# Beta folded into one decay exponent, the T-products evacuated by ScalarE, and a new order of the work on all engines of a fused delta-rule block

## The reference: what is computed

```
x = x + 0.5 * ffn(layernorm(x))       # r = sigmoid(xr Wr'), out = r * (relu(xk Wk')^2 Wv'), xr and xk mix each token with its predecessor
x = x +       attn(layernorm(x))
x = x + 0.5 * ffn(layernorm(x))
```

```
beta = sigmoid(h Wb');  g = -exp(A_log) * softplus(h Wa' + dt_bias)
S  = S * exp(g_t)
dv = (v_t - k_t S) * beta_t
S  = S + k_t (outer) dv
o  = q_t S
out = (o * rsqrt(mean(o*o) + 1e-5) * norm_w * silu(h Wg')) Wo'
```

## Time and profile before

| what | us |
|---|---|
| runs | 1873.60, 1883.21, 1891.46; median 1883.21 |
| the profiled execution's own time | 1883.35 |
| its span, first to last instruction | 1881.6 |
| busy PE, DVE, ACT, POOL | 1739.6, 1521.0, 1089.1, 438.4 |
| mean granted clock of TensorE | 0.965 of full |

### The profile page before, as it was taken

The page is one execution under the profiler, slowest core; times in us unless marked ns, Lnnn a source line. Parts: engine busy times, 40 slices in busy tenths (PEclk is TensorE's granted clock), DMA queues, the critical chain, the costliest instruction groups (busy, mean ns, idle before and its releaser), DMA issues.

```text
span 1881.6 us, 101829 instructions
## 1 busy us (share of the span) xinstructions
PE 1739.6 (92%) x45312; PEld 1486.7 (79%) x45312; DVE 1521.0 (81%) x4294; ACT 1089.1 (58%) x2002; POOL 438.4 (23%) x357
## 2 busy tenths in 40 slices
PE   5699999999999999999999999999999999999986
PEld 4587888787888788888888888888888878888775
DVE  4877889887888988888887888898788898887852
ACT  5556665555665565666565666555566555565533
POOL 0222221222221222222121222122222222222200
PEclk9889999999999999999999999999999999999877
DMA  3000000000000000000000000000000000000000
GB/s 113 2 3 4 15 14 4 15 14 15 15 15 9 9 15 15 15 15 15 3 15 14 15 15 15 9 9 14 15 15 15 9 9 9 9 9 10 9 9 13
DMA packets 21590, 26.50 MB, mean 14 GB/s; under 512 B 2209, under 2 KB 20769, under 8 KB 21153
## 3 DMA queue, kind: packets, MB, share of 16 engines
q1 hardware_dynamic: 21152, 19.99, 3.3%
HBM read 11.59 MB, written 8.39 MB: 11 GB/s over the span
## 4 chain that ended last, share of the span: by engine, by line
PE 53%; DVE 28%; issue 11%; ACT 1%; POOL 1%; DVEq 1%; ACTq 0%; POOLq 0%
PE ps L244 23%; PE ps L226 11%; PE ps L235 8%; DVE CV L1067 6%; DVE prod L1082 4%; DVE TZ L1083 3%; PE ps L219 2%; PE ps L400 2%; DVE T L1102 2%; PE ps L212 2%; DVE st L1035 2%; DVE XR L1056 1%; PE ps L357 1%; PE ps L461 1%; PE ps L372 1%
## 5 line engine op out<-in xcount | busy, mean ns | idle before, releaser
L1067 DVE SCALAR_TENSOR_TENSOR CV<-ps,cw,CV 128x256 f32<-128x256 f32 x576 | 250.8, 477 | 22.2 <-ACT CV L686 15.0
L244 PE MATMUL ps<-QE,S 64*64 64x16 f32 x4096 | 251.6, 209 | 2.0 <-ACT S L631 1.3
L244 PE MATMUL ps<-WP,V 64*64 64x16 f32 x4096 | 250.1, 208 | 0.0
L244 PEld LDWEIGHTS ps<-QE,S 64*64 64x64 f32 x4096 | 216.4, 138 | 35.0 <-issue 31.2
L244 PEld LDWEIGHTS ps<-WP,V 64*64 64x64 f32 x4096 | 217.4, 138 | 0.0
L244 PEld LDWEIGHTS ps<-WP,KD 64*64 64x64 f32 x4096 | 127.1, 137 | 36.5 <-DVE WP L1125 22.7
L1082 DVE TENSOR_TENSOR prod<-A,TZ 128x30 f32<-128x30 f32 (+7 forms) x480 | 139.0, 290 | 13.3
L967 POOL TENSOR_TENSOR OSQ<-OSQ,SQ 128x512 f32<-128x512 f32 x32 | 40.6, 1269 | 459.8 <-ACT OSQ L840 459.8
L244 PEld LDWEIGHTS ps<-SA,M 32*32 32x32 f32 x8192 | 91.0, 108 | 68.9 <-issue 34.3
L244 PE MATMUL ps<-SA,M 32*32 32x16 f32 x8192 | 117.9, 181 | 28.8 <-DVE SA L1096 18.4
L244 PE MATMUL ps<-KQI,K 64*64 64x48 f32 x4096 | 141.8, 221 | 1.4 <-DVE CV L1067 0.7
(11 more groups left out here) (152 smaller groups left out, 4055.4 us busy)
## 6 DMA issues: line engine op xcount, KB each, us to landing
X<-in_x SPq DMA_DIRECT2D x32, 256.0 KB, 2.9
out_x<-X SPq DMA_DIRECT2D x32, 256.0 KB, 2.3
KQI<-in_blocks SPq DMA_DIRECT2D x2, 256.0 KB, 4.2
w_r_ffn<-in_wT_r_ffn SPq DMA_DIRECT2D x1, 256.0 KB, 3.3
w_k_ffn<-in_wT_k_ffn SPq DMA_DIRECT2D x1, 256.0 KB, 3.5
w_v_ffn<-in_wT_v_ffn SPq DMA_DIRECT2D x1, 256.0 KB, 4.4
w_k<-in_wT_k SPq DMA_DIRECT2D x1, 256.0 KB, 4.3
w_q<-in_wT_q SPq DMA_DIRECT2D x1, 256.0 KB, 4.5
```

The source lines that it names most:

```text
L244: last = mm(ps[rows, o:o + n], stat[rows, pk].rearrange("p s c -> p (s c)"), mov[rows], **flags)
L1067: last = stt(d4[:, m], src, cw[:, i, m, tap:tap + 1], d4[:, m], ALU.mult, ALU.add)
```

## The change

What is computed stays the same. The parts:

- **One exponent.** `beta_diag` (GpSimd) writes log beta on the diagonal of a tile LD, and `stat1` becomes two operations, `stat0` and a subtraction, so that the statistic for `decay_steps` holds both g and log beta. `beta_in`, the tile EA, the second exp, `b_diag`, `b_reduce` and `beta_log` go. E now holds beta times the decay.
- **The gram step** multiplies both k·k and k·q by the same E in one 256-column operation (GK replaces AT and KP).
- **T on ScalarE.** `t_out0` and `t_out1` move from VectorE to ScalarE, three activations of 256 columns each, reading PSUM; no scaling by beta is left, two of the three scale by a 0/1 column.
- **Softplus.** `soft_exp` on ScalarE is now a chain of five: Abs, Exp, Identity (+1), Ln, Exp. VectorE keeps four operations of 64 columns and one of 32 (`soft_low`, `soft_part`, `soft_log`, `soft_max`, `gates`); the reciprocal goes.
- **Merged evacuation.** `d_out0` to `d_out3` write one tile MQ (384 columns in one operation) where M2 and QE took two; MQ has two buffers.
- **Finer segments.** The solve is issued as single multiplies and subtracts with other work between them, `t_product` and `b_product` in four parts, `o_product` in eight.
- **New order** on all engines but SyncE, and a new table `PS` of banks. ScalarE changes its table set twice in a step.

```diff
-PS = {"xt1": 2, "yt": 6, "xt3": 2, "r1": 0, ... "wo": 1, "g": 2, "dd": 5, ... "d1": 3, ... "t0": 0, "t1": 6, ...}
+PS = {"xt1": 5, "yt": 4, "xt3": 1, "r1": 2, ... "wo": 5, "g": 6, "dd": 4, ... "d1": 4, ... "t0": 4, "t1": 6, ...}
 # TensorE
-            def t_product1(g):
+            def t_product(g, q):
+                if q == 0:
+                    pe.wait_ge(s["tp"], g + 1)
...
+                for pk in range(q * RING, (q + 1) * RING):
+                    last = pairs(bk * BANK + pk % C * U, U, T2, pk, GK[:, pk, C:], start=True, stop=True)
...
             def d_product1(g):
...
+                if g < GROUPS - 2:
+                    pe.wait_ge(s["yt"], g + 3)
...
             def wo(g):
                 pe.wait_ge(s["ot"], g + 1)
...
-            def beta_in(g):
-                pe.wait_ge(s["lb"], g + 1)
-                pe.wait_ge(s["e"], g + 1)
-                for ub in range(M * B):
...
-                    last = mm(ps[:, o:o + P], LB[:, c0:c0 + P], ident, start=False, stop=(ub == M * B - 1), skip_group_check=True)
 # ScalarE
             def soft_exp(g):
...
+                own.done(af(ez[:], Z[:], ACT.Abs))
+                own.settle()
+                own.done(af(ez[:], ez[:], ACT.Exp, scale=-1.0))
+                own.settle()
+                own.done(af(uz[:], ez[:], ACT.Identity, bias=one))
+                own.settle()
+                own.done(af(lu[:], uz[:], ACT.Ln))
+                own.settle()
+                af(ru[:], lu[:], ACT.Exp, scale=-1.0).then_inc(s["ez"], 1)
...
+            def t_out0(g):
+                act.wait_ge(s["t_ps"], 4 * g + 2)
...
+                for h in range(2):
+                    own.done(af(WP[g % 2][:, rows, h * C:(h + 1) * C], src[:, :, C:U], ACT.Copy, scale=slot[:, h:h + 1]))
+                nc.scalar.copy(WP[g % 2][:, rows, U:], src[:, :, 0:C]).then_inc(s["wp"], 1)
 # GpSimd
+            def beta_diag(g):
+                pool.wait_ge(s["sp"], 5 * g + 5)
...
+                tt(packs(LD[:]), along(cz[:, BH:2 * BH]), over_packs(diag), ALU.mult).then_inc(s["ld"], 1)
             def stat1(g):
...
+                tt(ST[:], ST[:], LD[:], ALU.subtract).then_inc(s["stat1"], 1)
 # VectorE
             def d_out0(g):
...
-                own.done(tt(packs(QE[g % 2][:])[:, rows], packs(QP[:])[:, rows], src[:, :, U:], ALU.subtract))
-                tt(M2[:, rows].rearrange("p k s c -> p k (s c)"), GI2[:, rows], src[:, :, 0:U], ALU.subtract).then_inc(s["mt"], 1)
+                tt(MQ[g % 2][:, rows], GQ[:, rows], src, ALU.subtract).then_inc(s["mt"], 1)
             def gram0(g):
...
-                own.done(tt(packs(AT[:])[:, rows], src[:, :, 0:C], packs(EA[:])[:, rows], ALU.mult))
-                own.done(tt(KP[:, rows, C:U], src[:, :, C:U], packs(E[:])[:, rows], ALU.mult))
-                own.done(tt(KP[:, rows, 0:C], k_tok, along(packs(E[:])[:, rows, C - 1]), ALU.mult))
+                own.done(tt(GK[:, rows, 0:U].rearrange("p k (s c) -> p k s c", s=2), src[:, :, 0:U].rearrange("p k (s c) -> p k s c", s=2),
+                            vw(packs(E[:])[:, rows], [C, RING], [0, 2], [1, C]), ALU.mult))
+                own.done(tt(GK[:, rows, U:], k_tok, along(packs(E[:])[:, rows, C - 1]), ALU.mult))
```

More of the change, by code:

```diff
@@ L373, in q_proj, with b_product @@
                 last.then_inc(s["q_ps"], 1)
[L375 removed]
+            def b_product(g, q):
+                if q == 0:
+                    pe.wait_ge(s["wp"], 2 * g + 2)
+                    pe.wait_ge(s["vt"], g + 1)
+                if g and q == 0:
+                    pe.wait_ge(s["ch_s"], 8 * g)
                 w2 = WP[g % 2][:, :, 0:U].rearrange("p k (s c) -> p k s c", s=2)
[L377 removed]
+                for n in range(2 * q, 2 * q + 2):
                     for ub in range(M * B):
@@ L894, in _ @@
             ln_exp_set()
-            for step in range(GROUPS + 4):
-                on(square_k, step - 2)
+            for step in range(GROUPS + 5):
+                on(norm3, step - 5)
+                on(relu1, step - 1)
+                on(soft_exp, step - 2)
+                on(xt3, step - 5)
+                on(v_slots, step - 4)
+                silu_set()
+                on(gate, step - 2)
+                on(s_slots, step - 4)
+                on(relu3, step - 5)
+                on(silu_k, step - 2)
+                on(square_k, step - 2)
+                on(silu_v, step - 3)
+                on(tanh1, step - 1)
+                on(tap_v, step - 2)
+                on(tanh3, step - 5)
+                on(gates_wide, step - 2)
+                on(silu_q, step - 2)
@@ L897, in _ @@
                 ln_exp_set()
-                on(soft_exp, step - 2)
-                silu_set()
-                on(tanh1, step - 1)
+                on(k_root, step - 2)
+                on(rstd2, step - 1)
                 on(o_square, step - 4)
-                on(silu_v, step - 2)
+                on(norm2, step - 1)
+                on(exp_q, step - 2)
+                on(halo_y, step - 1)
+                on(t_out0, step - 3)
                 on(halo3, step - 4)
-                ln_exp_set()
@@ L905, in _ @@
                 on(o_root, step - 4)
-                on(halo1, step)
-                on(rstd1, step)
-                on(soft_ln, step - 2)
-                on(k_root, step - 2)
-                on(gates_wide, step - 2)
-                on(halo_y, step - 1)
-                on(rstd2, step - 1)
+                on(yt, step - 1)
+                on(square_q, step - 2)
+                on(t_out1, step - 3)
+                on(rstd1, step)
+                on(norm1, step)
+                on(tap_k, step - 1)
@@ L1519, in _ @@
                 on(gram1, step - 2)
+                on(mix_k3, step - 4)
                 on(chain, step - 3, 3)
-                on(mix_k3, step - 4)
+                on(gram2, step - 2)
                 on(chain, step - 3, 4)
-                on(mix_k1, step)
-                on(gram2, step - 2)
+                on(gram3, step - 2)
+                on(chain, step - 3, 5)
+                on(chain, step - 3, 6)
+                on(mix_r3, step - 4)
+                on(a_turn, step - 2)
+                on(solve_mul, step - 2, 0)
+                on(solve_sub, step - 2, 0)
+                on(solve_mul, step - 2, 1)
+                on(soft_low, step - 1)
+                on(solve_sub, step - 2, 1)
+                on(solve_mul, step - 2, 2)
+                on(soft_part, step - 1)
+                on(solve_sub, step - 2, 2)
+                on(solve_mul, step - 2, 3)
+                on(mix_r1, step)
+                on(chain, step - 3, 7)
+                on(solve_sub, step - 2, 3)
+                on(solve_mul, step - 2, 4)
+                on(solve_sub, step - 2, 4)
+                on(solve_mul, step - 2, 5)
+                on(solve_sub, step - 2, 5)
+                on(solve_mul, step - 2, 6)
+                on(solve_sub, step - 2, 6)
+                on(solve_mul, step - 2, 7)
+                on(solve_sub, step - 2, 7)
+                on(solve_mul, step - 2, 8)
 N_ZERO = 2
```

649 lines of the change are left out of this document (279 added, 370 removed), and 6 rows, old and new, of the table names.

## The result

| | median, us | runs |
|---|---|---|
| before | 1880.29 | 1873.60 to 1891.46, 4 runs |
| changed | 1809.48 | 1805.19 to 1813.92, 4 runs |

The ratio is 0.9618 [0.9561, 0.9675]: 3.8% faster, where 1834 us (2.6%) was forecast with a range of 1803 to 1880. So 1809 lies in the range, but not in the forecast's likeliest part (1815 to 1855, chance 0.55): it belongs to "more", under 1815, which had 0.13. In the profiled executions the span falls by 69.5 us, from 1881.6 to 1812.1. All ratios here leave out slow executions, one of the kernel before among them (2786 us at a granted clock of 0.541).

What follows compares the result with a forecast made beforehand. The prediction took TensorE's own work list to set the pace, with one standing wait, for OT. From 1883.35 us it took 35 for beta_in and 30 for OT and added 16 for new waits: 1834 us, range 1803 to 1880.

Steps and rivals of the forecast that it cites:

- 32 x 1.09 = 35 us less: TensorE's list: beta_in's products go, 1.09 us in each of 32 groups, counted in full as 35 us less.
- The wait for OT: TensorE's wait before the product with Wo, 30.2 us: goes but for tenths as OT comes earlier, -30 us.
- The new waits: Tight places in TensorE's new list, less an old wait of 0.2: about 0.5 us a step, +16 us.
- (a): d_product1 waits for ScalarE's copy of the second layernorm's transpose (YT): 0 to 0.5 us a step, taken as 0.2.
- (b): State chain's fourth link: VectorE's copy stands behind a gram step and mix_k3; wait 0 to 0.8 us, taken as 0.35.
- (c): State chain's links 5 and 6 stand back to back, as before: no change.
- The pauses and the cut runs: TensorE's 39.9 us of pauses without a cause the change removes stay; finer T-, b- and output segments add no product.
- more than forecast: Rival: shorter T- and b-runs halve the other pauses (-11), OT's wait goes in full (-48): 1800 us; chance 0.13.
- ScalarE as the bound: Rival: ScalarE's single file from k root to the copy delays d_product1 and Wo's product: 1905; chance 0.14, late solve included.
- the gain is given back by pauses: Rival: pauses come into the open and new waits reach 1 us a step: 1866 us; chance 0.18.
- The solve: T's transpose must be ready for the first T-product: VectorE 17.6 us against TensorE's 18.5, in time by 0.9.
- The rule weighed: Skill's drain of about 1.38 us per ScalarE table switch, before the k norm's root: 28 us more, 1862; chance 0.02.

Runs made afterwards that it cites:

- e8: Changed kernel with t_out0 and t_out1 (copying T out of PSUM) moved back from ScalarE to VectorE: 1811.65 us, 0.9565 of the kernel before.
- e12: The same kernel as e8, run again in more rounds: 1802.12 us, 0.9613 of the kernel before.
- e6: Kernel before with three of beta_in's four products left out: 1907.37 us, 1.0039 of the kernel before.
- e2: Changed kernel with the four products of decay_steps issued twice: 1820.88 us, 0.9653 of the kernel before.
- e9: Kernel before with soft_rest cut to one VectorE operation from the second group on: 1859.14 us, 0.9922 of the kernel before.
- e1: Kernel before with o_norm (OT) moved ahead of the gates and second layernorm's statistics in VectorE's list: 1897.05 us, 1.0056 of the kernel before.
- e10: Changed kernel with three unread ScalarE copies of 384 columns ahead of o_norm's root in every step: 1823.80 us, 0.9751 of the kernel before.
- e4: Changed kernel with the k projection and first b-quarter issued in turns, adding changes of tile size: 1837.75 us, 0.9728 of the kernel before.
- e3: Changed kernel with T-products in two runs instead of four and the second and third b-quarter joined: 1866.21 us, 0.9876 of the kernel before.
- e7: Changed kernel with only the first two T-quarters joined into one run: 1833.56 us, 0.967 of the kernel before.

## Why the prediction was right, and where it was not

**The bound was read rightly, in the main.** TensorE's list sets the step. It is 95% busy now, and of VectorE's 222 us less, priced at nothing by themselves, e8 and e12 give 64 back at no cost; the rest was not tried one by one. What the reading left out is that the list has also to be delivered, 256 instructions at a time. Of the signs named in advance, TensorE at 1715.9 us (1705), GpSimd at 474.5 (480) and the wait for OT at 3.8 (under 10) came out, VectorE at 1299.3 (1330), ScalarE at 1054.2 (1090) and the step at 52.91 (53 to 54.5) came out lower, and the wait of WP,KD for YT did not come.

**"32 x 1.09 = 35 us less" was too high by itself.** The rows of LB are gone, and TensorE's busy time per step fell by 1.20 us, which looks like the term. The two experiments say that it is not a toll paid in full: 0 of 22 us in the old order (e6, where two matmuls in 0.41 us are left of eight in 1.09), 7 to 20 of 28 in the new (e2). The step that failed is "nothing lies beside it on that engine": VectorE's copies for the chain and the delivery of the instructions lie beside it, and their waits take over what is taken away.

**The wait for OT, -30.** 26.4 us of it left the list. That it is worth its time where nothing else takes its place agrees with e9; that the old order had something in its place is shown by e1. In the changed kernel the wait went without a successor, which must come from the rest of the new order: not from T's copy on ScalarE, as e8 and e12 show, and perhaps from x1 and the gates standing earlier, which no run tried alone. This term holds, as part of the whole order and not as one move.

**The new waits, +16.** The list of the changed kernel has 1.6 us for YT, in 2 places, and 2.3 us more for SA: +4. For (a), 0.2 was taken per step, of 0 to 0.5; e10 finds 0.4 us of slack, so the true value is 0, by four tenths. The late copy of (b), taken as 0.35, is there in about half of the steps: the first row is the link behind two gram products, which waits so in 12 of the 23 middle steps, 0.17 us a step in the mean. The old wait of 0.2 behind the third link, in 14 of 23 steps and 0.12 a step, went as forecast, and so the two cancel. (c), the second row, is 0.36 in every step, before and now.

```profile
755.01 0.44 PE L241 MATMUL ps<-SA,MQ 32*32 32x16 f32 x32 [0.35 <-DVE SA L1105]
758.11 0.44 PE L241 MATMUL ps<-SA,MQ 32*32 32x16 f32 x32 [0.36 <-DVE SA L1105]
```

**The pauses and the cut runs, priced at 0.** This is the term that was mis-sized, and its reason was wrong: "those pauses have no cause that the change removes". Their cause is the delivery of TensorE's instructions, and wide products put between the smallest ones give it time. The forecast said that cutting the T-, b- and output products "adds no product", true, and cost nothing, false in both directions. It costs: the first T-half took 1.22 us in one piece (701.03 to 702.25) and takes 2 x 0.68 in two, and the sum of squares beside it 1.06 where it took 0.96. Over a step, the T- and b-products, the two sums of squares, the XN transposes and the decay sums, the same matmuls as before, take 0.86 us more from each start to the next, pauses and waits left out (means of 23 middle steps); the other products gave a part of it back. e4 has the price, 0.14 us for each change of tile size. And it pays: the pauses fell by 17.7 us, and with the long runs back, the kernel gives up 49 us (e3), pauses 29.4 of them in the profile. The rival "more than forecast" (1800) had named this, with -11 for it and a chance of 0.13; the result lies between the two, nearer to the rival.

**The sum.** For the 23 steps from the fifth to the 28th T transpose the two traces give this, in us per step; the half clock is what the distances from start to start are above their means at full clock.

| | forecast | in the traces |
|---|---|---|
| products of LB | -1.09 | -1.10 |
| wait for OT | -0.94 | -0.90 |
| new waits (forecast), waits for SA (traces) | +0.5 | +0.04 |
| pauses | 0 | -0.54 |
| half clock | 0 | -0.45 |
| all other products, at full clock | 0 | +0.53 |
| step | -1.53 | -2.42 |

This says where the time lay, not what each edit was worth; that is for the experiments. Without the short runs the other parts gave 1866 of 1890 us (e3), 24 less where 49 was forecast; the short runs gave the other 49. A toll that was not one and a saving put at nothing are errors against each other, and that the time fell into the range owes something to luck. e3 also moves some products and has a wait of its own (7.1 us), so the split is good to some 10 us.

**The clock.** In the middle window it rose from 0.99 to 1.00. Half-clocked stretches follow gaps, as in the earlier trace rows: in the kernel before each of the nine between 150 and 1720 us begins within 0.8 us of the end of a gap of 0.7 to 2.1 us, a pause or a wait for OT, though most such gaps have none behind them. One is left in the changed kernel between 132 and 1674 us:

```profile
697.85 0.30 PE L241 MATMUL ps<-SA,MQ 32*32 32x16 f32 x11 [1.33 <-issue]
698.08 3.60 PE L241 MATMUL ps<-KQI,K 64*64 64x48 f32 x64
```

The same products take 2.07 at 693.20. In 23 middle steps the loss by clock, (1 - clock) x step, fell from 0.59 to 0.07 us: some 16 us of the 76 (14 by the table's way of counting), and no term of mine had it. That it came with the gaps that went is read from their places, not tried. The clock over the whole span did not show this (0.965 to 0.967), as the stretch behind the last T transpose runs at 0.74 in the one and 0.66 in the other.

**The rivals.** ScalarE as the bound: price right (28.6 us for 0.95 us per step, against 31 per us), place right, but 0.4 us away from happening. That the gain is given back by pauses: no, since they fell. The solve: T's transpose ended at 722.14 and the first T-product began at 723.65, 1.5 us of margin where 0.9 was worked out.

**The rule weighed.** A table load begins at 719.89 and takes 1.28; the next activation starts at 721.78, 0.61 behind it, and waited for TensorE's sum:

```profile
719.89 1.28 ACT L624 ACT_TABLE_LOAD   x1
721.78 0.69 ACT L831 ACTIVATE SK<-ps,headp 128x512 f32<-128x512 f32 x1 [0.61 <-PE ps L544]
```

The drain of about 1.38 us that the Trainium skill, ScalarE: Activation LUTs, section "What ACT_TABLE_LOAD costs", adds does not fit into 0.61 either; by the trace the load is its 1.28 us.

## What to carry to other kernels

Where an engine alternates between waits of tenths and pauses of a microsecond, do not price a piece of removed work at its duration: ask which wait inherits it, and try the removal alone. When a pause has no name, count the engine's instructions up to it and look at the DMA queue that brings them, before calling it causeless. Here 256 instructions of TensorE done in less than some 3 to 4 us end in a pause, so long products belong between the smallest ones; cutting runs of 128 to 64 was worth more (49 us) than leaving out beta_in's products, 2% of TensorE's time, could have been (35), at a price of 0.14 us per change of tile size. A wait for one engine is worth its time only if the work that it is swapped with has no waiter of its own.

## What the hardware showed that was not expected

- **TensorE pauses for its own instructions.** They come in transfers of 16384 bytes, 256 instructions each, and a group's first instruction never ran sooner than 1.12 us after its transfer's end; 652 of the 674 pauses of the fourteen traces stand there. They read 22.2, 31.1, 51.6 us as one, then all T-runs were lengthened (changed kernel, e7, e3), and only 12.3, 16.7 and 10.2 where wide products were added or spread (e2, e4) or a wait for YT stands in most steps (e10), since time spent on anything else within the 256 comes off the pause.
- **Less work, longer steps.** With 0.7 us of TensorE's work per step left out, no time was gained, and in the profiles the step grew from 55.36 to 56.26 us and the clock fell from 0.965 to 0.948 (e6; two chips).
- **VectorE beside GpSimd.** x1's second operation (X<-XR,X, 128x512) took 1488 ns in the mean before, where GpSimd's GS product ran beside it, and 692 in the changed kernel and in e9, where none does. The Trainium skill, GPSIMD Engine Reference, section "Specifications", says that GpSimd shares its SBUF interfaces with VectorE and contends with its instructions of two SBUF inputs; this one has two, and the trace agrees.
- **The end varies from one execution to the next.** From the last T transpose to the end the changed kernel took 86.4 us at a mean clock of 0.66 in one profile and 78.6 at 0.74 in another. So 8 us between two profiled spans can come from there alone, which is why the steps are compared.
